# Experts' stage of a sparse layer: TensorE's program written out, with one register load per block

## The chip, the cores and the metric

The kernel runs on one core of a Trainium2 chip. The metric is the device time of one execution in microseconds (us); for a kernel it is the median of several runs. One execution of each kernel is also recorded by the hardware profiler, and all rows shown here are from that one.

## The reference

The input is a float32 tensor of 4 x 2048 tokens with 256 channels, and all products are to be computed at float32 accuracy. Cut to what matters:

```python
x = x + layernorm(attn(layernorm(x), w_lin))      # a convolution of 31 taps, its weights a softmax per token and head
x = x + layernorm(ffn(layernorm(x), ...))

def ffn(x):                                       # x: 8192 tokens x 256
    shared = silu(x @ shared_w_gate.T) * (x @ shared_w_up.T) @ shared_w_down.T      # inner width 704
    shared = shared * sigmoid(x @ shared_gate_w.T)
    rw, sel = top_k(softmax(x @ gate_w.T), 2)     # 2 of 16 experts for each token
    combine = scatter(rw / rw.sum(-1), sel)
    g, h = split(einsum('nd,edf->nef', x, w_gate_up))      # 128 + 128 columns per expert
    out = einsum('nef,efd,ne->nd', silu(g) * h, w_down, combine)
    return out + shared
```

The change lies in the last two lines of the experts' part: the products with `w_gate_up` and `w_down`.

## The kernel before, in words

The program has four stages with a barrier of all engines between them: attention; routing together with a first part of the shared network; the experts; the rest of the shared network with the combination of everything (`shared_and_combine`).

Routing sorts the 16384 pairs of token and expert by expert and cuts them into blocks of 128 rows, each for one expert only; NBK is 144 blocks. It leaves in SBUF the row numbers of each block (`ids`) and, in a row of int32 on one partition, the expert of each block (`block_expert`, with 12 zeros behind the 144 values). The weights of all 16 experts are held in SBUF too, each as two float32r tensors: `eh` holds the rounded values and `el` what rounding left. A product at float32 accuracy is then made of three: high by high, high by low, low by high.

The experts' stage (`experts`, from line 1111) works through the blocks like this:

- GpSimd gathers the 128 rows of a block (`xg`, an indirect DMA, line 806), up to eight blocks ahead.
- TensorE transposes them (`turn_x`, two transposes, line 1184). ScalarE rounds the result to `xh` (line 1234), and VectorE forms the rest `xl` (line 1252).
- TensorE multiplies by gate and up weights (`gate_up`, line 1208): for each half `c` of the channels three products, six in all. The weights loaded into the array are the rows of x; what streams through is the expert's slice of `eh` or `el`, at an address computed from the register that holds the expert's number.
- ScalarE takes the silu (line 1238) and VectorE the product (line 1256). TensorE transposes that (`turn_h`, line 1215), and ScalarE and VectorE split it into `ehh` (line 1242) and `ehl` (line 1260).
- TensorE multiplies by the down weights (`down`, three products, line 1222). VectorE copies the result out (line 1265) and SyncE stores it (line 1162).

The order is written out by hand. A step n does, on TensorE, `turn_x` of block n + 2, `turn_h` of block n - 1, `gate_up` of block n + 1 and `down` of block n - 2, in this order. So `gate_up` of a block comes one step after its `turn_x`, and `down` of a block three steps after its `gate_up`. Each engine has the same helper, `steps` (line 1137): the steps -2 to 1 are written out, then a hardware loop of 17 turns holds eight steps each (R = 8), then the steps 138 to 145 are written out again. Line 1140 is the loop itself. GpSimd alone has no loop.

TensorE needs each block's expert number in a register. Before, it loads twelve registers at once (`load_experts`, line 1189): before the first step, at the beginning of each turn of the loop and once behind the loop, 19 loads in all. `find` hands out the loaded registers to the blocks. A turn needs eight new ones and four that the steps before had already (for `down` of the last blocks).

Of the kernel before, what the change touches and what calls it, by code (L numbers as in the profile page):

```python
# [32 lines left out]
FF, E, MF = 704, 16, 128  # L33
# [8 lines left out]
NBK = NBLK + 1  # L42
# [762 lines left out]
def gather_rows(nc, to, yn_d, ids, b):  # L805
    return nc.gpsimd.indirect_dma_start(out=to, out_offset=None, in_=yn_d.rearrange("n p c -> (n p) c"),  # L806
                                        in_offset=bass.IndirectOffsetOnAxis(ap=ids[:, b:b + 1], axis=0))
# [303 lines left out]
def experts(nc, eh, el, xg, xg_in, x_full, ids, first_d, yn_d, yg_d, ident, ones, block_expert, pb):  # L1111
    with ExitStack() as ctx:
        def sb(name, shape, dt=F32):
            return ctx.enter_context(nc.sbuf_tensor(name, shape, dt))

        def sem(name):
            return ctx.enter_context(nc.semaphore(name))
        R = 8
        xg2 = sb("xg2", [P, R // 2, C])
        xh = sb("xh", [P, 2, C], F32R)  # L1120
        xl = sb("xl", [P, 2, C], F32R)
        sg = sb("esg", [P, 2, P])
        hm = sb("ehm", [P, 2, P])
        hh = sb("ehh", [P, 2, P], F32R)
        hl = sb("ehl", [P, 2, P], F32R)
        yo = sb("yo", [P, R, C])
        names = "xh_ok xl_ok gu_full sg_ok hm_ok ht_full hh_ok hl_ok y_full yo_ok".split()
        s = {n: sem("e_" + n) for n in names}
        s["x_full"] = x_full
        yo_out = [sem(f"e_yo_out{k}") for k in range(R)]  # L1130
        block = ctx.enter_context(nc.Block())
        px, pg, ph, py = pb[0:2], pb[2:4], pb[4:6], pb[6:8]
        AHEAD = R - 2
        FROM = 2
        TO = FROM + (NBK - AHEAD - FROM) // R * R

        def steps(eng, step, enter=None):
            for n in range(-2, FROM):
                step(n, n % R)
            with eng.Fori(0, (TO - FROM) // R) as i:  # L1140
                if enter:
                    enter(i * R + FROM, FROM % R)
                for u in range(R):
                    step(i * R + FROM + u, (FROM + u) % R)
            if enter:
                enter(TO, TO % R)
            for n in range(TO, NBK + 2):
                step(n, n % R)

        def rows(r):  # L1150
            return xg[:, r] if r < R // 2 else xg2[:, r - R // 2]

        def parts(n, r, *work):
            for ahead, f in work:
                if not isinstance(n, int) or 0 <= n + ahead < NBK:
                    f(n + ahead, (r + ahead) % R)

        @block.sync
        def _(sp):
            def store(b, r):  # L1160
                sp.wait_ge(s["yo_ok"], b + 3)
                sp.dma_start(yg_d[bass.ds(b * P, P)] if not isinstance(b, int) else yg_d[b * P:b * P + P], yo[:, r]
                             ).then_inc(yo_out[r], 16)
            for k in range(R):
                sp.dma_start(first_d[k], ones[:, 0:4]).then_inc(yo_out[k], 16)
            steps(sp, lambda n, r: parts(n, r, (-2, store)))
            for k in range(R):
                sp.wait_ge(yo_out[k], 16 + NBK // R * 16)

        @block.gpsimd  # L1170
        def _(po):
            for b in range(R // 2, NBK):
                if b >= R:
                    po.wait_ge(s["x_full"], b + 1)
                gather_rows(nc, rows(b % R), yn_d, ids, b).then_inc(xg_in[b % R], 16)

        @block.tensor
        def _(pe):
            pe.sem_inc(s["x_full"], R)

            def turn_x(b, r):
                pe.wait_ge(xg_in[r], (b - r) * (16 // R) + 16)
                for c in range(CC):
                    ins = nc.tensor.transpose(px[r % 2][:, c * P:(c + 1) * P], rows(r)[:, c * P:(c + 1) * P], ident[:])  # L1184
                ins.then_inc(s["x_full"], 1)
            held, loaded = {}, []

            def load_experts(b):
                loaded[:] = nc.values_load_multi_w_load_instructions(
                    block_expert[0:1, bass.ds(b, R + 4)], engines=(mybir.EngineType.PE,), min_val=0, max_val=E - 1,  # L1190
                    skip_runtime_bounds_check_because="routing clamps every block's expert to 0 .. E - 1")[1]

            def find(_, r):
                if loaded:
                    held[r] = loaded.pop(0)

            def enter(n, r):
                load_experts(n - 2)
                for k in range(-2, 2):
                    find(n + k, (r + k) % R)  # L1200

            def gate_up(b, r):
                e = held[r]
                pe.wait_ge(s["xl_ok"], b + 3)
                j = 0
                for c in range(CC):
                    for a, w in ((xh, eh), (xh, el), (xl, eh)):
                        ins = nc.tensor.matmul(pg[r % 2][:, 0:2 * MF], a[:, r % 2, c * P:(c + 1) * P],  # L1208
                                               w[:, bass.ds(e, 1), c * C:(c + 1) * C], start=(j == 0), stop=(j == 5))
                        j += 1  # L1210
                ins.then_inc(s["gu_full"], 1)

            def turn_h(b, r):
                pe.wait_ge(s["hm_ok"], b + 3)
                nc.tensor.transpose(ph[r % 2][:, 0:P], hm[:, r % 2], ident[:]).then_inc(s["ht_full"], 1)

            def down(b, r):
                e = held[r]
                pe.wait_ge(s["hl_ok"], b + 3)
                pe.wait_ge(s["yo_ok"], b + 1)  # L1220
                for j, (a, w) in enumerate(((hh, eh), (hh, el), (hl, eh))):
                    ins = nc.tensor.matmul(py[r % 2][:, 0:C], a[:, r % 2], w[:, bass.ds(e, 1), 2 * C:3 * C],
                                           start=(j == 0), stop=(j == 2))
                ins.then_inc(s["y_full"], 1)
            load_experts(0)
            steps(pe, lambda n, r: parts(n, r, (2, turn_x), (-1, turn_h), (1, gate_up), (-2, down), (2, find)), enter)

        @block.scalar
        def _(act):
            act.preload_act_table(ACT.Silu)  # L1230

            def x_high(b, r):
                act.wait_ge(s["x_full"], b + 1 + R)
                nc.scalar.activation(xh[:, r % 2], px[r % 2][:, 0:C], ACT.Copy).then_inc(s["xh_ok"], 1)  # L1234

            def silu(b, r):
                act.wait_ge(s["gu_full"], b + 1)
                nc.scalar.activation(sg[:, r % 2], pg[r % 2][:, 0:MF], ACT.Silu).then_inc(s["sg_ok"], 1)

            def h_high(b, r):  # L1240
                act.wait_ge(s["ht_full"], b + 1)
                nc.scalar.activation(hh[:, r % 2], ph[r % 2][:, 0:P], ACT.Copy).then_inc(s["hh_ok"], 1)
            steps(act, lambda n, r: parts(n, r, (2, x_high), (-1, h_high), (1, silu)))

        @block.vector
        def _(ve):
            for name in ("xl_ok", "hm_ok", "hl_ok", "yo_ok"):
                ve.sem_inc(s[name], 2)

            def x_low(b, r):  # L1250
                ve.wait_ge(s["xh_ok"], b + 1)
                nc.vector.tensor_tensor(xl[:, r % 2], px[r % 2][:, 0:C], xh[:, r % 2].bitcast(F32), ALU.subtract).then_inc(s["xl_ok"], 1)  # L1252

            def gated(b, r):
                ve.wait_ge(s["sg_ok"], b + 1)
                nc.vector.tensor_tensor(hm[:, r % 2], sg[:, r % 2], pg[r % 2][:, MF:2 * MF], ALU.mult).then_inc(s["hm_ok"], 1)

            def h_low(b, r):
                ve.wait_ge(s["hh_ok"], b + 1)
                nc.vector.tensor_tensor(hl[:, r % 2], ph[r % 2][:, 0:P], hh[:, r % 2].bitcast(F32), ALU.subtract).then_inc(s["hl_ok"], 1)  # L1260

            def leave(b, r):
                ve.wait_ge(s["y_full"], b + 1)
                ve.wait_ge(yo_out[r], (b - r) * (16 // R) + 16)
                nc.vector.tensor_copy(yo[:, r], py[r % 2][:, 0:C]).then_inc(s["yo_ok"], 1)
            steps(ve, lambda n, r: parts(n, r, (2, x_low), (-1, h_low), (1, gated), (-2, leave)))
# [203 lines left out]
```

## Time and profile before

| | us |
|---|---|
| median of 3 runs | 1089.03 (1088.56 to 1089.05) |
| the profiled execution | 1088.95 |
| its span, first to last instruction | 1086.9 |
| TensorE matmuls busy | 959.6 (88%) |
| VectorE busy | 861.3 (79%) |
| ScalarE busy | 557.3 (51%) |
| GpSimd busy | 489.6 (45%) |

The span is a little shorter than the time of the execution, as what lies before the first and after the last instruction isn't in it. Busy time is the sum of the durations of an engine's instructions, without overlaps. PE is TensorE's matmuls and PEld its weight loads; they overlap, and matmuls are pipelined, so two that start 0.12 us apart can each have a duration of 0.28 us. The start times tell the pace.

### The profile page before, as it was taken

The page shows a single profiled execution, that of the slowest core. Times are in us where ns is not written, and L with a number is a line of the kernel's source. Part 1 is how long each engine was busy: PE and PEld are TensorE (multiplying, and loading weights), DVE is VectorE, ACT ScalarE, POOL GpSimd, SP SyncE. Part 2 cuts the span into 40 slices and gives each one's busy share as a digit, 9 for nine tenths or more (in the row PEclk, how much of TensorE's full clock was granted, in tenths as well). Part 3 has the DMA queues.
Part 4 walks back from the last instruction along what each step waited for, and adds up shares of the span by engine and source line. Part 5 has one row for each costly group of instructions (what it writes and reads, how often), then busy time and mean ns, then how long its engine had stood idle before and what let it go on. Part 6 is the DMA issues. An engine that isn't in the chain of part 4 may idle for free. (4 is left out here: it accounts for less than half of the span.)

```text
span 1086.9 us, 27047 instructions
## 1 busy us (share of the span) xinstructions
PE 959.6 (88%) x9256; PEld 843.6 (78%) x9257; DVE 861.3 (79%) x2402; ACT 557.3 (51%) x1314; POOL 489.6 (45%) x715
## 2 busy tenths in 40 slices
PE   5998898998899768887897999999998799999995
PEld 4767787886788657766676998999987688888884
DVE  5977998797999668888885688788884578878777
ACT  5994445899144532333235455555553345554553
POOL 4452556421355400000002665566644786777762
PEclk9998999999899769899989899999999899999998
DMA  5532678633468630221123655555575465555541
GB/s 170 170 96 70 185 228 253 197 123 84 116 191 241 204 117 15 79 72 49 49 68 107 153 172 170 165 168 171 171 156 174 150 180 175 175 169 189 157 145 49
DMA packets 154723, 156.86 MB, mean 144 GB/s; under 512 B 52480, under 2 KB 134528, under 8 KB 154624
## 3 DMA queue, kind: packets, MB, share of 16 engines
q1 hardware_dynamic: 136048, 112.40, 33.5%
q0 software_dynamic: 13056, 35.67, 12.3%
q10 hardware_dynamic: 5520, 7.47, 2.3%
q8 instruction: 62, 1.02, 0.4%
q14 instruction: 37, 0.30, 0.1%
HBM read 91.38 MB, written 64.11 MB: 143 GB/s over the span
## 5 line engine op out<-in xcount | busy, mean ns | idle before, releaser
L806 POOL DMA_INDIRECT xg<-yn_scratch,ids x144 | 136.9, 951 | 282.9 <-DVE ids L1046 188.0
L1334 POOL DMA_INDIRECT cy<-expert_rows,slots x128 | 146.1, 1141 | 54.1 <-issue 35.8
L765 PE MATMUL bank<-yh,gh 128*128 128x512 f32 x352 | 144.8, 411 | 19.4 <-DVE s_hf L745 9.1
L647 PE MATMUL bank<-xbd,am 128*32 128x68 f32 x4096 | 138.2, 304 | 11.0 <-DMA xbd<-xn_scratch 6.6
L765 PE MATMUL bank<-yl,gh 128*128 128x512 f32 x352 | 142.3, 404 | 0.0
L765 PE MATMUL bank<-yh,gl 128*128 128x512 f32 x352 | 141.9, 403 | 0.0
L647 PEld LDWEIGHTS bank<-xbd,am 128*32 128x32 f32 x4096 | 122.8, 129 | 18.5 <-issue 8.8
L765 PEld LDWEIGHTS bank<-yh,gh 128*128 128x128 f32 x352 | 68.8, 195 | 33.8 <-DVE s_hf L745 7.9
L1208 PE MATMUL bank<-eh,xh 128*128 x288 | 94.0, 327 | 0.6 <-DVE xl L1252 0.6
L1252 DVE TENSOR_TENSOR xl<-bank,xh 128x256 fp32r<-128x256 f32 x144 | 61.1, 424 | 34.1 <-ACT xh L1234 27.0
L1234 ACT ACTIVATE xh<-bank 128x256 fp32r<-128x256 f32 x144 | 55.2, 384 | 61.5 <-PE bank L1184 61.0
L436 DVE TENSOR_TENSOR am<-probs,mask 128x512 f32<-128x512 f32 x128 | 80.0, 687 | 8.4 <-ACT probs L529 7.6
L1208 PE MATMUL bank<-el,xh 128*128 x288 | 83.0, 288 | 0.0
L725 ACT ACTIVATE s_hh<-s_hf 128x512 fp32r<-128x512 f32 (+1 forms) x36 | 22.7, 632 | 115.8 <-DVE s_hf L745 115.8
L1208 PE MATMUL bank<-eh,xl 128*128 x288 | 81.7, 284 | 0.0
L765 PEld LDWEIGHTS bank<-yh,gl 128*128 128x128 f32 x352 | 68.6, 195 | 16.9
L765 PEld LDWEIGHTS bank<-yl,gh 128*128 128x128 f32 x352 | 68.8, 195 | 12.3
L543 ACT ACTIVATE av<-av,shift,rstd 128x256 f32<-128x256 f32 x64 | 35.0, 594 | 82.7 <-POOL shift L347 82.7
L780 PE MATMUL bank<-dh,c_hh 128*128 128x256 f32 x240 | 67.3, 285 | 9.8 <-DVE c_hh L751 9.5
L368 POOL TENSOR_TENSOR x<-av,xr 128x256 f32<-128x256 f32 x64 | 46.9, 754 | 63.0 <-ACT yn L552 59.7
L725 ACT ACTIVATE c_hh<-c_hf 128x512 fp32r<-128x512 f32 (+1 forms) x60 | 38.0, 633 | 71.9 <-DVE c_hf L745 71.9
L745 DVE TENSOR_TENSOR c_hf<-c_sg,bank 128x512 f32<-128x512 f32 (+1 forms) x60 | 41.2, 687 | 42.0 <-ACT c_sg L723 41.5
(191 smaller groups left out, 2865.7 us busy)
## 6 DMA issues: line engine op xcount, KB each, us to landing
expert_rows<-yo SPq DMA_DIRECT2D x144, 128.0 KB, 1.8
xbd<-xn_scratch SPq DMA_DIRECT2D x128, 72.0 KB, 2.3
xt<-xp SPq DMA_DIRECT2D x32, 256.0 KB, 2.7
xn_scratch<-xn SPq DMA_DIRECT2D x64, 128.0 KB, 2.7
xr<-x SPq DMA_DIRECT2D x32, 256.0 KB, 3.6
x_scratch<-x SPq DMA_DIRECT2D x32, 256.0 KB, 3.5
yn_scratch<-yn SPq DMA_DIRECT2D x32, 256.0 KB, 3.7
ynt_scratch<-ynt SPq DMA_DIRECT2D x32, 256.0 KB, 4.4
```

What stands on the lines that cost most here:

```text
L368: nc.gpsimd.tensor_tensor(x2[:, q, t], av[:, q, t], xr[:, q, t], ALU.add).then_inc(s["x2_ok"], 1)
L436: nc.vector.tensor_tensor(am[:, q, g], probs[:, bass.ds(i * CB, CB), g, None, :].to_broadcast([P, CB, 2, J]), mask[:, None].to_broadcast([ ...
L647: ins = nc.tensor.matmul(pso[q][t][J * b:J * b + J, g * MW:(g + 1) * MW], am[:, q, g, e, side], xbd[:, q, e + side, :, g], start=(g == 0 a ...
L725: self.nc.scalar.activation(self.hh[0:f, g], self.hf[0:f, k], ACT.Copy).then_inc(self.s["hh_ok"], 1)
L745: self.nc.vector.tensor_tensor(self.hf[0:f, k], self.sg[0:f, k], up, ALU.mult).then_inc(self.s["hf_ok"], 1)
L765: ins = self.nc.tensor.matmul(self.pb[2 * k + half][:], w[:, c, col:col + P], y[:, n % 2, c, :], start=(j == 0), stop=(j == 5))
L780: ins = self.nc.tensor.matmul(o, a[:, g, t * P:(t + 1) * P], w[:, m, :], start=(m == 0 and t % 2 == 0 and j == 0), stop=(m == FT - 1 and j ...
L806: return nc.gpsimd.indirect_dma_start(out=to, out_offset=None, in_=yn_d.rearrange("n p c -> (n p) c"), in_offset=bass.IndirectOffsetOnAxis ...
L1208: ins = nc.tensor.matmul(pg[r % 2][:, 0:2 * MF], a[:, r % 2, c * P:(c + 1) * P], w[:, bass.ds(e, 1), c * C:(c + 1) * C], start=(j == 0), s ...
L1234: nc.scalar.activation(xh[:, r % 2], px[r % 2][:, 0:C], ACT.Copy).then_inc(s["xh_ok"], 1)
L1252: nc.vector.tensor_tensor(xl[:, r % 2], px[r % 2][:, 0:C], xh[:, r % 2].bitcast(F32), ALU.subtract).then_inc(s["xl_ok"], 1)
L1334: nc.gpsimd.indirect_dma_start(out=y[:, r, t, j], out_offset=None, in_=yg_d, in_offset=bass.IndirectOffsetOnAxis(ap=slots[:, 2 * unit + t, ...
```

## The change

TensorE no longer uses `steps`: its 148 steps are written out. Thresholds of its waits become constants by that. A load of one register comes before the first step; then each `gate_up` holds the load for the next block, between its third and fourth product. `load_experts` and `enter` go. All other engines keep their loops, and what is computed stays the same.

```diff
-        def steps(eng, step, enter=None):
+        def steps(eng, step):
             for n in range(-2, FROM):
                 step(n, n % R)
             with eng.Fori(0, (TO - FROM) // R) as i:
-                if enter:
-                    enter(i * R + FROM, FROM % R)
                 for u in range(R):
                     step(i * R + FROM + u, (FROM + u) % R)
-            if enter:
-                enter(TO, TO % R)
             for n in range(TO, NBK + 2):
                 step(n, n % R)
...
-            held, loaded = {}, []
-
-            def load_experts(b):
-                loaded[:] = nc.values_load_multi_w_load_instructions(
-                    block_expert[0:1, bass.ds(b, R + 4)], engines=(mybir.EngineType.PE,), min_val=0, max_val=E - 1,
-                    skip_runtime_bounds_check_because="routing clamps every block's expert to 0 .. E - 1")[1]
-
-            def find(_, r):
-                if loaded:
-                    held[r] = loaded.pop(0)
-
-            def enter(n, r):
-                load_experts(n - 2)
-                for k in range(-2, 2):
-                    find(n + k, (r + k) % R)
+            held = {}
+
+            def find(b):
+                held[b] = nc.values_load_multi_w_load_instructions(
+                    block_expert[0:1, b:b + 1], engines=(mybir.EngineType.PE,), min_val=0, max_val=E - 1,
+                    skip_runtime_bounds_check_because="routing clamps every block's expert to 0 .. E - 1")[1][0]
 
             def gate_up(b, r):
-                e = held[r]
+                e = held[b]
                 pe.wait_ge(s["xl_ok"], b + 3)
                 j = 0
                 for c in range(CC):
...
                                                w[:, bass.ds(e, 1), c * C:(c + 1) * C], start=(j == 0), stop=(j == 5))
                         j += 1
+                        if j == 3 and b + 1 < NBK:
+                            find(b + 1)
                 ins.then_inc(s["gu_full"], 1)
...
             def down(b, r):
-                e = held[r]
+                e = held.pop(b)
...
-            load_experts(0)
-            steps(pe, lambda n, r: parts(n, r, (2, turn_x), (-1, turn_h), (1, gate_up), (-2, down), (2, find)), enter)
+            find(0)
+            for n in range(-2, NBK + 2):
+                parts(n, n % R, (2, turn_x), (-1, turn_h), (1, gate_up), (-2, down))
```

## Rows read from the trace of the kernel before

**Rows 1.** The page: its first line and engine busy times.

```profile
span 1086.9 us, 27047 instructions
...
PE 959.6 (88%) x9256; PEld 843.6 (78%) x9257; DVE 861.3 (79%) x2402; ACT 557.3 (51%) x1314; POOL 489.6 (45%) x715
```

**Rows 2.** Engines by stretches: stretch, length, busy of each, PEclk, DMA share, GB/s.

```profile
100.00:150.00 50.00, 44.95 (x1189) 40.85 (x1184) 47.84 (x139) 18.65 (x48) 28.39 (x51) 1.00 0.67 186
150.00:200.00 50.00, 45.19 (x864) 39.81 (x857) 41.97 (x132) 28.82 (x80) 30.88 (x69) 0.93 0.82 249
...
606.00:815.00 209.00, 194.41 (x1625) 190.31 (x1624) 168.50 (x543) 112.25 (x406) 124.97 (x133) 1.00 0.58 168
```

**Rows 3.** Who waited for whom, 596 to 826 us: total, times, longest.

```profile
POOL xg L806 <- PE bank L1184: 75.3, 122, 2.1
...
PEld bank L1184 <- issue: 22.9, 18, 4.8
```

**Rows 4.** Timeline of TensorE's weight loads: start, us, line; idle time before it.

```profile
617.28 0.20 PEld L1184 LDWEIGHTS bank<-ident,xg 128*128 128x128 f32 x2 [1.15 <-issue]
...
621.49 0.25 PEld L1184 LDWEIGHTS bank<-ident,xg 128*128 128x128 f32 x2
...
622.88 0.25 PEld L1184 LDWEIGHTS bank<-ident,xg 128*128 128x128 f32 x2
...
623.56 0.19 PEld L1208 LDWEIGHTS bank<-eh,xh 128*128 128x128 f32 x1
...
624.29 0.24 PEld L1184 LDWEIGHTS bank<-ident,xg 128*128 128x128 f32 x2
...
627.07 0.24 PEld L1184 LDWEIGHTS bank<-ident,xg 128*128 128x128 f32 x2
...
628.34 0.19 PEld L1222 LDWEIGHTS bank<-eh,ehl 128*128 128x128 f32 x1
629.65 0.20 PEld L1184 LDWEIGHTS bank<-ident,xg 128*128 128x128 f32 x2 [1.13 <-issue]
...
803.33 0.20 PEld L1184 LDWEIGHTS bank<-ident,xg 128*128 128x128 f32 x2 [1.06 <-issue]
```

**Rows 5.** Line 1189 in several stretches: ns min/median/max, first and last start (us).

```profile
L1189 PEldq TENSOR_LOAD <-block_expert x19: 852/1072/1851, 596.1 to 814.3; - x19
...
L1189 PEldq TENSOR_LOAD <-block_expert x1: 1851/1851/1851, 596.1 to 596.1; - x1
...
L1189 PEldq TENSOR_LOAD <-block_expert x1: 872/872/872, 603.4 to 603.4; - x1
...
L1189 PEldq TENSOR_LOAD <-block_expert x1: 1095/1095/1095, 628.4 to 628.4; - x1
...
L1189 PEldq TENSOR_LOAD <-block_expert x11: 1054/1073/1095, 628.4 to 752.4; - x11
```

**Rows 6.** The chain that ended last, behind the stage: start, us, what.

```profile
827.59 0.94 POOL cy L1334
...
869.52 3.20 issue
```

**Rows 7.** Timeline of weight loads behind the loop.

```profile
815.13 0.20 PEld L1184 LDWEIGHTS bank<-ident,xg 128*128 128x128 f32 x2 [0.49 <-issue]
```

**Rows 8.** The sequencer's own instructions, by line, in three stretches and in all.

```profile
L1208 PEldq FUSED_REGOPS  x2: 46/46/46, 624.3 to 624.5; - x2
...
L1208 PEldq FUSED_REGOPS  x2: 46/46/46, 816.5 to 816.7; - x2
...
L1222 PEldq ALU_OP  x1: 32/32/32, 817.2 to 817.2; - x1
...
L1140 PEldq COMPARE_BRANCH  x17: 83/215/232, 615.6 to 814.1; - x17
```

**Rows 9.** Timeline of VectorE, the low part of x.

```profile
623.83 0.42 DVE L1252 TENSOR_TENSOR xl<-bank,xh 128x256 fp32r<-128x256 f32 x1
...
630.54 0.42 DVE L1252 TENSOR_TENSOR xl<-bank,xh 128x256 fp32r<-128x256 f32 x1 [1.19 <-ACT xh L1234]
```

## The prediction

> **What bounds the kernel now.** I read the page first: 1086.9 us of span, with TensorE busy for 88% of it, more than any other engine [rows 1]. Then I read stretches, because the change touches one stage alone. The experts' stage runs from about 596 to 826 us; between 606 and 815 us TensorE is busy 194.4 of 209.0 us and its granted clock is 1.00, that is 2.4 GHz [rows 2]. So something takes 7% of TensorE's time there, and the view of who waited for whom names it: 18 waits of the weight loads ahead of the transposes of line 1184, put down to "issue", 22.9 us [rows 3]. The reader should see that no other engine is named: TensorE's own instruction stream is late. The other row says who follows whom: GpSimd waits for the same transposes 122 times, so its gathers go at TensorE's pace.
>
> The timeline shows the pattern. Inside a turn of the loop, the first transpose of one step and that of the next start 1.39 to 1.40 us apart (621.49, 622.88, 624.29); across the loop's edge it is 2.58 us (627.07 to 629.65), with 1.13 us in which no weight load runs [rows 4]. In that gap stands one instruction of line 1189, the load of twelve registers: 1.095 us from 628.4 [rows 5]. It begins when the queue ahead of the array holds the last products only (the last weight load starts at 628.34), so nearly all of it is bare. The stage ends in a barrier, and behind it GpSimd's gathers start at 827.59 and carry the chain until TensorE takes over near 870 [rows 6]. Nothing there began before the barrier, so a shorter or longer experts' stage moves the end by the same amount.
>
> **Part by part, the removed edges.** First transposes at the sixteen turns' edges start at 617.28, ..., 803.33: fifteen intervals, 186.05 / 15 = 12.40 us for eight blocks [rows 4]. Eight dense steps are 8 x 1.395 = 11.16 us (627.07 less 621.49 is 5.58 us for four). An edge costs 1.24 us, sixteen cost 19.9 us. The seventeenth load, behind the loop, leaves a gap of 0.49 us [rows 7]: 0.5 us. The load at the loop's entry (603.4, 0.87 us [rows 5]) costs nothing: at half clock a block of products lasts longer than it. Sum of what can go: 20.4 us. The very first load is on the path too: 1.85 us with TensorE idle [rows 5]. One register in place of twelve saves between 0 and 1.8 us of it; it is the first of its kind and cold, so I take 0.3 us.
>
> **Thresholds and branches.** The register arithmetic for waits and the branch itself (0.22 us in the median, 0.08 where not taken [rows 8]) are issued while the sequencer has time to spare, or are in the 1.24 us already. Written-out code has no such arithmetic: 0 us, between -0.1 (sequencer's slack gone) and 0. The longer program must be fetched; the attention stage, which is also written out, runs 1189 matmuls and 1184 weight loads in 50 us, 47 a microsecond [rows 2], and a block here needs 24 with some ten register instructions in 1.39 us, 25 a microsecond. 0 us, and up to 1 us if a fetch comes late now and then.
>
> **The other engines' loops** stay. Today their edges fall near TensorE's gap; later they fall amid dense work. The low part of x ends at 624.25 and the first products of the next step are released at 624.3 [rows 8, 9], with their weight load some 0.1 to 0.3 us later, so a hundred nanoseconds lost by VectorE's branch can reach TensorE. Seventeen edges by 0 to 0.15 us: 0 to 2.5 us, I take 0.8 us.
>
> **The new loads** decide. There are 144 of them, one per block, in place of 19. Each sits between the third and the fourth product of a block; the sequencer does nothing else while it lasts, so the question is its duration, X. No row has a load of one register. Bounds from the nearest rows: twelve registers took 0.85 us at least (the last one, with no gathers beside it) and 1.07 us in the median of the nineteen [rows 5]. If the price is all per register, X is 0.07 to 0.09 us; if none of it is, 0.85 to 1.07 us.
>
> What a given X does is a cycle over two steps. (1) From the release of a block's products (sequencer) to the load: 0.24 us, the distance of the two address instructions of line 1208 (816.5, 816.7 [rows 8]). (2) The load, X. (3) From the load's end to the next weight load with one address instruction between: 0.15 us, as 629.50 to 629.65 today [rows 4, 5]. (4) Fourth product to the next transpose: 0.72 us (623.56 to 624.29 [rows 4]). (5) Transpose, ScalarE's copy, VectorE's difference, release of the step after: 629.65 to 630.96 and some 0.04 us, 1.35 us where nothing presses [rows 4, 9]. Two periods are at least 0.24 + X + 0.15 + 0.72 + 1.35, so the period is at least 1.23 + X/2. I add 0.02 for the dense case, where step 5 takes 1.40 us (622.88 to 624.3): 1.25 + X/2. The sequencer alone needs 0.84 us for a block (816.5 to 817.2, and the pushes of three transposes), and 0.06 us around a load: 0.90 + X. TensorE's own work is 1.395 us. The period is the largest of the three.
>
> So up to X = 0.29 us the load is free: the queue and the chain cover it. Above it each 0.1 us costs 0.05 us a block, 7 us over 141 blocks, and above 0.70 us twice that. The gain of 20.4 us is eaten when the period reaches 1.395 + 20.4/141 = 1.540 us, at X = 0.58 us.
>
> Which X? The eleven loads between 628 and 753 us lie between 1.054 and 1.095 us [rows 5], and are 0.2 us longer than the quiet one. Twelve small delays add up to so narrow a band more easily than one round trip under traffic does. I take a twelfth of 1.07, 0.09 us, and a fixed part like that of the other control instructions with work in them, 0.08 to 0.22 us [rows 8]: X = 0.25 us.
>
> The Trainium skill speaks against this, and its pages against each other. "DMA: Bandwidth & Descriptors", section "Latency and other measured facts", has a floor of about 600 ns for a tensor load; by it the sum would be a small loss, about 2 us, and more under traffic. "Runtime: NRT & Kernel Launch", section "Instruction fetch mechanics", has about 200 ns per register; by that twelve would take 2.4 us, and the trace has 0.85 to 1.10 once warm, so as a figure it does not hold here, though its kind of cost (per register) is the one that I take.
>
> **Sum.** -19.9 - 0.5 - 0.3 + 0.8 + 0 (loads, fully covered, since 1.25 + 0.125 is under 1.395) = -19.9 us. The profiled execution took 1088.95 us, 2.05 us more than its span; 1088.95 - 19.9 = 1069.05 us. The median of the runs is 1089.03, 0.08 above. As the cover at X = 0.25 is thin (0.04 us from its end) I add 0.7 us (a period longer by 0.005 us, 141 times): 1069.8 us.
>
> **The rivals.**
> - *The load is mostly a fixed price.* Two thirds or more of the quiet 0.85 us, so X is 0.63 us up to 0.85. The period is then 1.565 us, and 1.75 us at the top by the sequencer. (1.565 - 1.395) x 141 = 24.0, less 20.4: +4 us, 1093 us; at the top 50.1 - 20.4 = +30 us, 1119 us; with 1.07 us even the period 1.97 and +61 us, 1150 us. It decides from X = 0.58 us. For it: the first load took 1.85 us, so a load is no plain register instruction. Against it: the narrow band. TensorE would also be busy only 89% or less; stretches of attention busy 45.2 of 50 us were granted 0.93 [rows 2], which could add some us. The skill's floor of a tensor load, named above, is this rival.
> - *Half and half.* X between 0.30 and 0.53 us: a period of 1.40 to 1.515 us, +1 to +17 us on -20.4: 1069 to 1086 us.
> - *The edges' gain isn't kept*: with the gap gone VectorE or GpSimd sets the pace. GpSimd's gather takes 0.94 us with 0.3 between two, waiting 75.3 us in all for TensorE [rows 3], so it could go at 1.25 us; VectorE is busy 168.5 of 209.0 us [rows 2], 81%, and 87% of a stage shortened to 195. The price would be all of 20 us, 1089 us. Little speaks for it.
>
> **How the numbers follow.** Chances: forecast (X up to 0.30) 0.47; half and half 0.14; X of 0.53 to 0.63, which lands within 2 us of before, 0.07; mostly fixed 0.30; gain not kept 0.02. No change here means within 0.2%, 2.2 us, about what a measurement of this kernel can tell. Faster is 0.47 + 0.14 less 0.01 = 0.60, within 0.2% 0.07 + 0.02 = 0.09, slower 0.31 (0.30 and 0.01 for a clock that falls). The range begins at 1066 us (the first load saves 1.8, the other edges cost nothing) and reaches to the fixed price at X = 0.7 us, 1.60 us a step, +9 us: 1098 us. Left out are some 0.03 below and 0.16 above. Forecast's own range: 1066 to 1074 us.
>
> **What would show it.** A row of TENSOR_LOAD for one register, x144: near 0.25 us is right, 0.6 and more is the first rival. First transposes 1.39 to 1.42 us apart all through, with no gap at every eighth. Waits on "issue" ahead of line 1184 down from 18 to 1 or 2. If instead the fourth product of each block starts late by some hundred nanoseconds and the steps lie 1.5 us or more apart, step 2 of the cycle was longer than I take. Gaps of TensorE put down to VectorE's xl at every eighth block would show the other loops' edges. The stages ahead of 596 us and behind the barrier must have the same lengths; if not, the sum is wrong in its frame.

## The result, and the profile after

The changed kernel takes 1080.39 us in the median of five runs (1078.07 to 1083.44), the kernel before 1089.05 (1088.56 to 1089.88): a ratio of 0.9925, interval 0.9904 to 0.9945. It is faster by 0.75%, where 1.8% was forecast.

The page of the changed kernel, first line and engines:

```profile
span 1078.5 us, 26898 instructions
...
PE 965.1 (89%) x9256; PEld 847.5 (79%) x9256; DVE 861.5 (80%) x2402; ACT 557.2 (52%) x1314; POOL 491.1 (46%) x715
```

The change did what it says. The waits on "issue" ahead of the transposes (now line 1180) fell from 18 to the one at the stage's start. In their place stand 15 ahead of the products of line 1195. The view of waits of the changed kernel, 596 to 826 us:

```profile
PEld bank L1195 <- issue: 4.4, 15, 1.0
PEld bank L1180 <- issue: 4.0, 1, 4.0
```

That view shows only the gaps in which no weight load ran. The loss is greater and lies in the steps' length, from the first transpose of one step to that of the next. This is the timeline of its weight loads:

```profile
688.86 0.24 PEld L1180 LDWEIGHTS bank<-ident,xg 128*128 128x128 f32 x2
...
689.42 0.19 PEld L1195 LDWEIGHTS bank<-eh,xl 128*128 128x128 f32 x1
689.93 0.19 PEld L1195 LDWEIGHTS bank<-eh,xh 128*128 128x128 f32 x1 [0.33 <-issue]
...
690.64 0.24 PEld L1180 LDWEIGHTS bank<-ident,xg 128*128 128x128 f32 x2
...
692.07 0.24 PEld L1180 LDWEIGHTS bank<-ident,xg 128*128 128x128 f32 x2
```

The weight loads of a block's third and fourth product start 0.51 us apart here instead of 0.12, and the step takes 1.78 us (688.86 to 690.64); the next takes 1.43. What stands between is one register load, 0.517 us from 689.3. First its row, then all 144, then those before and from 607 us on (line 1185 of the changed kernel; ns min/median/max):

```profile
L1185 PEldq TENSOR_LOAD <-block_expert x1: 517/517/517, 689.3 to 689.3; - x1
...
L1185 PEldq TENSOR_LOAD <-block_expert x144: 297/382/1088, 597.9 to 811.2; - x144
...
L1185 PEldq TENSOR_LOAD <-block_expert x6: 298/304/1088, 597.9 to 606.5; - x6
...
L1185 PEldq TENSOR_LOAD <-block_expert x138: 297/384/564, 608.0 to 811.2; - x138
```

So X is 0.30 us in the first blocks and 0.30 to 0.56 us later, 0.40 us on the mean of blocks 10 to 137. Those rows answer to [rows 5]. The busy share warns of nothing. Engines of the changed kernel between 606 and 806 us:

```profile
606.00:806.00 200.00, 199.28 (x1620) 193.82 (x1619) 167.45 (x540) 111.90 (x405) 126.47 (x134) 1.00 0.62 177
```

TensorE is "busy" for 199.3 of 200 us, against 194.4 of 209 in [rows 2], while a step takes 1.485 us on the mean instead of the 1.395 inside a turn of the loop before. A product's record lasts 0.28 us where two start 0.12 us apart, and the late fourth one has 0.38, so most of the delay is hidden under records. Counting blocks per microsecond tells the pace, the share does not.

The time by parts, from starts in both traces: first to last block's transpose, 221.26 us before and 211.95 after (-9.3); the first load 1.85 and 1.09 (-0.8); up to the barrier ahead of the stage +1.8, in code that the change does not touch; from the last transpose to the end 267.6 and 267.5 (-0.1). Together -8.4 us, the difference of the spans.

### The profile page after: what moved, and what is told of

Its sections match the earlier page's. It is cut to its first block and busy times, and to the rows that moved or that the text cites. A ratio compares the mean times of both kernels' runs of the same rounds, so it can differ in the third digit from the quotient of the medians.

```text
span 1078.5 us, 26898 instructions
## 1 busy us (share of the span) xinstructions
PE 965.1 (89%) x9256; PEld 847.5 (79%) x9256; DVE 861.5 (80%) x2402; ACT 557.2 (52%) x1314; POOL 491.1 (46%) x715
## 5 line engine op out<-in xcount | busy, mean ns | idle before, releaser
L1195 PE MATMUL bank<-eh,xh 128*128 x288 | 100.1, 348 | 1.5 <-DVE xl L1242 0.8
```

## The experiments

Times of one kernel differ between chips by some us, so each run is compared by its ratio with the kernel before on the same chip. Where no ratio is given there is a single execution, and only its trace is read. "Stage" is the time from the first to the last block's first transpose; the lines of the transposes give it. "Steps" are those of blocks 10 to 137. The edits are cut to what matters.

**No loads at all.** All blocks use the register of the first.

```diff
-                e = held[b]
+                e = held[0]
...
-                        if j == 3 and b + 1 < NBK:
-                            find(b + 1)
...
-                e = held.pop(b)
+                e = held[0]
```

> Leaves out all loads of an expert's number but the first: every block is multiplied with the first block's expert. The instructions are otherwise those of the changed kernel. Theory A: steps of 1.395 us throughout, the 0.089 us that a step has on the mean beyond that times 137 steps go, 12 us: 1068 us. This is also the term of 20 us for the removed edges by itself. Theory C: the steps stay near 1.48 us or are late at every eighth, 1075 to 1080 us.

Measured: 1068.43 us, 0.9810 (0.9770 to 0.9849). Each step takes 1.392 to 1.400 us. The transposes' row, of this kernel and of the changed one:

```profile
L1180 PEld LDWEIGHTS bank<-ident,xg x288: 137/139/224, 598.0 to 798.8; 128*128 128x128 f32 x144
```

```profile
L1180 PEld LDWEIGHTS bank<-ident,xg x288: 137/140/224, 599.0 to 811.1; 128*128 128x128 f32 x144
```

The stage is 200.6 us, 20.6 less than before and 11.3 less than with the loads. So the edges were worth what was forecast, the other engines' loops (in the kernel before, VectorE's branch takes 0.05 to 0.07 us) and the fetching of the long program cost nothing that can be seen, and the loads cost 11.3 us.

**The load ahead of the wait for xl.**

```diff
                 e = held[b]
+                if b + 1 < NBK:
+                    find(b + 1)
                 pe.wait_ge(s["xl_ok"], b + 3)
...
-                        if j == 3 and b + 1 < NBK:
-                            find(b + 1)
```

> The one-register load moves from between the third and fourth product to ahead of gate_up's wait for xl, behind the pushes of the transposes. Theory A (the cycle: a load delays only what follows it in TensorE's program, and its price is what sticks out of time in which the sequencer has nothing to do): the sequencer waits there for xl some 0.45 us of every step, the load has a mean of 0.39 us, so it is covered but for the longest ones; steps of 1.395 to 1.41 us, 1068 to 1071 us. Theory B (a load costs its price wherever it stands, because it stops the queue ahead of the array): 1080 us, as with the load amid the products. Theory C (what was lost comes from the other engines' loop edges or from fetching the written-out code): 1078 to 1081 us too, with late steps at every eighth.

Measured: 1066.39 us, 0.9813 (0.9780 to 0.9847). Stage 199.8 us, steps of 1.392 to 1.400 us: as without any load. The number of loads is the same; only their place differs. Its transposes and its loads from 608 us:

```profile
L1180 PEld LDWEIGHTS bank<-ident,xg x288: 137/139/229, 593.4 to 793.2; 128*128 128x128 f32 x144
...
L1185 PEldq TENSOR_LOAD <-block_expert x133: 296/301/440, 608.4 to 792.6; - x133
```

B and C fall. The loads are also shorter here, 0.306 us on the mean, which no theory had said. So this run by itself leaves open how much is the place and how much the shorter load; the runs without stores and with chosen counts, below, part the two.

**Two loads amid the products.** The line `find(b + 1)` stands twice.

> Two loads of one register, one behind the other, between the third and the fourth product, X = 0.85 us instead of 0.39. Theory A: the period is the larger of 1.25 + X/2 = 1.675 us and 0.90 + X = 1.75 us, so 0.27 us more in 141 steps: 1118 us. A straight line through no load and one load (12 us for 0.39 us) gives 1094 us instead.

Measured: 1079.82 us, 0.9931 (0.9909 to 0.9953). It tests nothing: the trace holds 144 loads, not 287, so the unused one had gone from the program. As a repetition of the changed kernel it gives its time again.

```profile
L1185 PEldq TENSOR_LOAD <-block_expert x144: 296/382/1090, 593.0 to 807.9; - x144
```

**Behind the down products**, ahead of the next step's transposes.

```diff
-                parts(n, n % R, (2, turn_x), (-1, turn_h), (1, gate_up), (-2, down))
+                parts(n, n % R, (2, turn_x), (-1, turn_h), (1, gate_up), (-2, down), (2, lambda b, r: find(b) if b else None))
```

> The one-register load stands behind the down products, ahead of the next step's transposes. Theory A in its mended form (a load's time counts in full only between the release of a block's products and the next transposes, when it stands amid products that the array hasn't in its queue; elsewhere the sequencer's 0.5 us of spare time in a step take it): 0.31 + 0.06 us fit in, steps of 1.395 us, 1066 to 1069 us. Rival (the load delays the transposes, and by the chain over two steps half of it comes out as with the load amid the products): steps near 1.45 us, 1078 us.

Measured: 1068.78 us, 0.9809 (0.9778 to 0.9840), steps of 1.392 to 1.400 us, stage 199.6 us. The mended theory holds: two places around the wait are free for a load of 0.31 us, the one amid the products is not.

**Writing out alone**: batches of twelve (`find` now loads R + 4 registers) at the old place, and none amid the products.

```diff
-                    block_expert[0:1, b:b + 1], engines=...
+                    block_expert[0:1, b:b + R + 4], engines=...
...
-                        if j == 3 and b + 1 < NBK:
-                            find(b + 1)
...
+                if FROM <= n <= TO and (n - FROM) % R == 0:
+                    find(n - 2)
                 parts(n, n % R, (2, turn_x), (-1, turn_h), (1, gate_up), (-2, down))
```

> TensorE's program written out, but the loads as before the change: twelve registers at once ahead of every eighth step, at the place of the loop's edge. Tells the writing-out from the placing of loads. Theory A (the queue ahead of the array runs dry because of the load): branch and loop arithmetic go, so the load starts some 0.45 us earlier while the queue is still fuller, and 16 edges keep 1.24 - 0.45 = 0.8 us each: 1081 us, steps of 1.395 us between. Rival (the edge is the branch's price: after a taken branch the code must be fetched anew, and the load's 1.07 us beside the 0.85 us of the one behind the loop is that too): the load falls to 0.85 us and the edges keep 0.5 us or less: 1076 us.

Measured: 1074.11 us, 0.9878 (0.9855 to 0.9900), better than the change itself. Its loads, then its timeline at an edge:

```profile
L1185 PEldq TENSOR_LOAD <-block_expert x17: 844/849/867, 612.5 to 795.9; - x17
```

```profile
634.57 0.24 PEld L1180 LDWEIGHTS bank<-ident,xg 128*128 128x128 f32 x2
...
635.84 0.19 PEld L1210 LDWEIGHTS bank<-eh,ehl 128*128 128x128 f32 x1
636.29 0.20 PEld L1180 LDWEIGHTS bank<-ident,xg 128*128 128x128 f32 x2 [0.27 <-issue]
...
637.65 0.24 PEld L1180 LDWEIGHTS bank<-ident,xg 128*128 128x128 f32 x2
```

The edge's two steps take 1.72 and 1.36 us; 3.08 less 2.79 leaves 0.3 us for an edge, 1.24 before. Both theories have a part, and a third thing went that neither had. The starts of the sequencer's instructions give it: from the last address instruction of a step to the load 0.11 us instead of 0.60 (branch and loop arithmetic), the load 0.85 us instead of 1.07, from the load's end to the release of the next products 0.08 us instead of 0.39 (register arithmetic for the waits). Whether the load is shorter for want of a taken branch, as the rival has it, or because it meets no store (below), no run shows for the batch.

**The loop kept, its batch moved** behind the turn's first transposes.

```diff
+                if due:
+                    enter(*due.pop())
                 e = held[r]
                 pe.wait_ge(s["xl_ok"], b + 3)
...
-            steps(pe, lambda n, r: parts(...), enter)
+            steps(pe, lambda n, r: parts(...), lambda n, r: due.append((n, r)))
```

> The kernel before with one edit: the loop stays, and its load of twelve registers moves from ahead of the turn's first transposes to between them and the wait for xl. Theory A: the sequencer has some 0.45 us to spare there and the queue holds the transposes, so an edge costs about 0.6 us instead of 1.24: 1078 us. If place did not matter: 1088 us.

Measured: 1089.27 us, 1.0006 (0.9987 to 1.0024): no gain. Its loads and the edge:

```profile
L1189 PEldq TENSOR_LOAD <-block_expert x16: 974/1055/1274, 613.7 to 799.6; - x16
```

```profile
626.16 0.14 PEld L1219 LDWEIGHTS bank<-ident,ehm 128*128 128x128 f32 x1
627.37 0.19 PEld L1212 LDWEIGHTS bank<-eh,xh 128*128 128x128 f32 x1 [1.06 <-issue]
```

The gap only moved behind the transposes. I had counted the sequencer's spare 0.45 us for the load, but at an edge the loop's own instructions (add, branch of 0.22 us, address) stand ahead and spend it. From the last address instruction of a step to the release of the next products it takes 2.08 us on the mean at the edges of the kernel before, 2.06 here and 1.05 in the written-out run, and an edge costs 1.24, 1.24 and 0.30 us. So in all three some 0.8 us of that distance are free and the rest counts, on whichever side of the transposes the load stands. Writing out shortens the distance by branch and arithmetic, and so frees the time that hides a load. A loop that keeps its branch and has one-register loads ahead of the wait was not tried.

**What makes the load longer.** Stores held back until behind the last block:

```diff
-                sp.dma_start(yg_d[...], yo[:, r]).then_inc(yo_out[r], 16)
+                sp.sem_inc(yo_out[r], 16)
...
+            for b in range(NBK):
+                sp.dma_start(yg_d[b * P:b * P + P], yo[:, b % R]).then_inc(late, 16)
```

> The changed kernel without SyncE's stores while the blocks are worked on: all 144 are issued in a burst behind the last block, from whatever the buffers then hold, so its whole time says nothing. Looked at: the duration of the one-register loads, 0.30 us in the first ten and 0.30 to 0.56 us from then on. If the stores' traffic is what the load meets, it is 0.30 us throughout and the steps fall to about 1.44 us; if it is the gathers', it stays as it was, 0.39 us on the mean.

And no gathers after the first eight blocks:

```diff
-            for b in range(R // 2, NBK):
-                if b >= R:
-                    po.wait_ge(s["x_full"], b + 1)
+            for b in range(R // 2, R):
...
-                pe.wait_ge(xg_in[r], (b - r) * (16 // R) + 16)
+                if b < R:
+                    pe.wait_ge(xg_in[r], 16)
```

> The changed kernel with the gathers of the first eight blocks alone; the later blocks use their rows again. Looked at: the duration of the one-register loads. If the gathers are what the load meets: 0.30 us throughout, steps of about 1.44 us by the cycle as measured (1.285 + X/2), TensorE's stage 7 us shorter: 1074 us. If the stores are: 0.39 us as before.

Each is a single execution, for its trace. The loads without stores, then without gathers:

```profile
L1188 PEldq TENSOR_LOAD <-block_expert x140: 295/301/316, 600.2 to 799.3; - x140
```

```profile
L1184 PEldq TENSOR_LOAD <-block_expert x135: 297/435/564, 608.2 to 809.8; - x135
```

It is the stores (128 KB from SBUF per block). Without them X is 0.30 us throughout, and the step takes 1.431 us on the mean, 1.436 by the measured cycle below; the stage takes 204.9 us (the whole 1139.86 us, with the stores in a burst at the end). Without gathers X stays long, 0.44 us on the mean, the step takes 1.504 us and the whole 1079.3 us. So of the 11.3 us that the loads cost, 4.3 are a load of 0.30 us at this place, and 7.0 its lengthening by stores.

Why the place matters to X too is read from the traces alone, no run moved the stores. Amid the products a load starts 0.57 to 0.86 us behind the start of a store's issue, and 101 of 134 take over 0.33 us; ahead of the wait it starts mostly 1.15 to 1.37 us behind, and 5 of 134 do. The batches at the written-out edge start 1.2 us behind a store and take 0.85 us; those of the loop start 0.2 to 0.3 us behind, last through the busy time and take 1.07 us in the median.

**The price by the number of registers.** First amid the products, in turn 1, 2, 4 and 8 from places 4k, 4k + 1, 4k + 2, 4k + 3; the whole took 1165.09 us, where 1090 was expected.

```diff
+                k = (1, 2, 4, 8)[b % 4]
                 held[b] = nc.values_load_multi_w_load_instructions(
-                    block_expert[0:1, b:b + 1], engines=...
+                    block_expert[0:1, b:b + k], engines=...
```

> The loads at their place take 1, 2, 4 and 8 registers in turn, of which the first alone is used. Price per register from twelve at 1.07 and one at 0.39 us: 0.062 us. So 0.39, 0.45, 0.58, 0.82 us if the price is a fixed part of 0.33 us and an equal one for each register; a step at some count (all of one fetch for one price) would show as two equal durations. Time near 1090 us by the cycle (mean X 0.56 us).

```profile
L1186 PEldq TENSOR_LOAD <-block_expert x1: 322/322/322, 600.5 to 600.5; - x1
...
L1186 PEldq TENSOR_LOAD <-block_expert x1: 535/535/535, 602.7 to 602.7; - x1
...
L1186 PEldq TENSOR_LOAD <-block_expert x1: 1107/1107/1107, 605.3 to 605.3; - x1
...
L1186 PEldq TENSOR_LOAD <-block_expert x1: 2158/2158/2158, 607.3 to 607.3; - x1
```

A miss: eight registers take about 2 us where twelve had taken 0.85. So the counts were taken again with the places chosen, ahead of the wait:

> The loads stand ahead of the wait for xl and take 12, 1, 2, 2, 4, 4, 2, 1, 8, 1, 2, 2, 4, 4, 2, 1 registers in turn, from the block's own place in the list; the first alone is used. Loads of 2, 4 and 8 that began at odd places took 0.24 us for each register more; twelve that began at a multiple of eight took 0.85 us. If the price goes by pieces of 16 bytes that a load touches, loads of 4, 8 and 12 from a multiple of four take some 0.35, 0.6 and 0.85 us, and those of 4 from an odd place 1.0 us. If it goes by the number of registers alone, 4 take 1.0 us wherever they begin and 8 take 1.95, and twelve at 0.85 us stay unexplained. The whole time says little.

Four from 12, four from 13, eight from 24, twelve from 16, two from 18:

```profile
L1186 PEldq TENSOR_LOAD <-block_expert x1: 339/339/339, 613.7 to 613.7; - x1
...
L1186 PEldq TENSOR_LOAD <-block_expert x1: 1002/1002/1002, 615.0 to 615.0; - x1
...
L1186 PEldq TENSOR_LOAD <-block_expert x1: 601/601/601, 632.1 to 632.1; - x1
...
L1186 PEldq TENSOR_LOAD <-block_expert x1: 857/857/857, 619.9 to 619.9; - x1
...
L1186 PEldq TENSOR_LOAD <-block_expert x1: 547/547/547, 622.9 to 622.9; - x1
```

From a place that is a multiple of four, 4, 8 and 12 registers take 0.34, 0.60 and 0.86 us: 0.26 us for each four (16 bytes) and 0.08 fixed. Others take some 0.23 us for each register and 0.07 fixed: 0.30, 0.54, 1.00. In 11 of the 16 positions at least eight of the nine loads agree within 0.03 us; three positions of two registers and the two of four from an odd place spread more, by 0.08 to 0.41 us. A group of four costs about what one register does.

This run also says how much is hidden ahead of the wait. Two of its steps, with twelve registers (0.86 us from 619.9) and with eight (0.60 us from 632.1):

```profile
620.31 0.25 PEld L1180 LDWEIGHTS bank<-ident,xg 128*128 128x128 f32 x2
...
621.94 0.24 PEld L1180 LDWEIGHTS bank<-ident,xg 128*128 128x128 f32 x2
...
632.55 0.24 PEld L1180 LDWEIGHTS bank<-ident,xg 128*128 128x128 f32 x2
...
633.95 0.24 PEld L1180 LDWEIGHTS bank<-ident,xg 128*128 128x128 f32 x2
```

The first takes 1.63 us, the second 1.40. From block 17 on all eight loads of eight registers (0.59 to 0.60 us) and all 32 of two that don't follow a long one (0.53 to 0.64 us) leave steps of 1.39 to 1.40 us; the seven of twelve (0.85 to 0.87 us) have steps of 1.58 to 1.65 us. So it is the place that makes a load free there, up to 0.6 us of it, and not its being short: theory A holds. Amid the products 0.30 us already cost something (1.431 us a step without stores).

**The best version**: ahead of the wait, and the very first load behind the first transposes. Against the run with the load ahead of the wait:

```diff
+                if b == 0:
+                    find(0)
                 e = held[b]
                 if b + 1 < NBK:
                     find(b + 1)
                 pe.wait_ge(s["xl_ok"], b + 3)
...
-            find(0)
```

> The load ahead of the wait for xl as in the best run so far, and the very first load (1.08 us, ahead of the stage's first transposes) moved behind the first two blocks' transposes, where TensorE waits 1.4 us for xl anyway. Theory A: 1.0 us less than with the load ahead of the wait alone, 1065 to 1067 us; visible in the trace as the distance from the barrier to the first transpose, less in a time of runs that spread by 3 us. If the first products come later by as much, nothing is gained.

Measured: 1065.84 us, 0.9792 (0.9768 to 0.9816). From TensorE's arrival at the barrier to the first product it takes 5.9 us instead of 6.7 (the run with the load ahead of the wait). In time the two can't be told apart. Either beats both kernels.

## Why the prediction was wrong

The direction and the cycle over two steps were right, the size was not. The spans differ by -8.4 us: the edges -20.6, the first load -0.8, the new loads +11.3, the stages ahead +1.8, behind -0.1.

- *Removed edges, -20.4 us*: right. Without loads the stage is 20.6 us shorter, with whatever the other engines' loops cost in it.
- *First load, -0.3 us*: -0.8 us; cold, one register takes 1.09 us.
- *Other engines' loops, +0.8 us*: nothing measurable; VectorE's branch takes 0.05 to 0.07 us, and the steps of the run without loads have no late eighth.
- *Thresholds, branches, fetching, 0 us*: held as a term of its own, with one thing missed. I put branch and arithmetic among what the 1.24 us of an edge contains and did not see how large their share is: written out with the very same batches, an edge keeps 0.3 us. Branch and loop arithmetic take 0.49 us of the sequencer there, the arithmetic for the waits 0.31, the longer load 0.22.
- *The new loads, 0 us (0.7 with the margin)*: this is the step that failed. They cost 11.3 us. X was taken as 0.25 us and is 0.40, and the cover that I gave it ended at 0.29. The cycle itself is the right one. Its terms, means of blocks 10 to 137 of the changed kernel, with the forecast's in brackets: release to load 0.26 (0.24); load 0.40 (0.25); load's end to the fourth product 0.17 (0.15); fourth product to the next transposes 0.73 (0.72); transposes to release 1.41 (1.39). The sum is 2.97 us for two steps, 1.485 for one, and 1.485 us is what the trace has. Forecast were 2.75 and so 1.375, under TensorE's own 1.395. Of the 0.11 us between, 0.075 are X, and 0.035 the small rest. That small rest also moved the end of the cover: the period is 1.285 + X/2 with the measured terms, and passes 1.395 at X = 0.22 us, so that even the 0.25 us forecast would not have been free.

The five terms follow one another around two steps, so their sum is two steps whatever the mechanism. What bears the cycle out is, first, that four of them stay the same within 0.01 us when X changes: with X of 0.30 us (no stores), 0.40 (the changed kernel) and 0.44 (no gathers) the step takes 1.431, 1.485 and 1.504 us. Second, in 118 of the 128 blocks the release comes within 0.06 us behind the end of VectorE's xl; in the other ten the sequencer itself is late. One such release, at 692.04 us, 0.04 us behind the end of xl (VectorE's timeline, then the sequencer's row of line 1195):

```profile
691.58 0.42 DVE L1242 TENSOR_TENSOR xl<-bank,xh 128x256 fp32r<-128x256 f32 x1
...
L1195 PEldq FUSED_REGOPS  x1: 46/46/46, 692.0 to 692.0; - x1
```

It is also the sign that the prediction named for a load that is too long: the fourth product late by some hundred nanoseconds.

Why was X wrong? I took a twelfth of the batch's price for one register. The batch behaves as if it were read in three aligned pieces of 0.26 us; a single register costs almost a piece and the fixed part, 0.30 us. The bounds (0.07 to 1.07 us) held it; my choice inside them rested on a narrow band that said nothing on this question. And 0.10 us more comes from the stores; the same rows had two prices for a batch (0.85 and 1.07 us) without my asking at which moment of a step the new loads would fall.

The rival "half and half" (X from 0.30 to 0.53 us, 1069 to 1086 us), with 0.14, is what happened. The range held the median.

Of the two rules of the Trainium skill: the floor of about 600 ns for a tensor load ("DMA: Bandwidth & Descriptors", "Latency and other measured facts") does not hold for this load from SBUF, which takes 0.30 us. The 200 ns per register ("Runtime: NRT & Kernel Launch", "Instruction fetch mechanics"), which the page gives for the runtime's own register loads, is near the 0.23 us of registers read one by one here, though not near aligned groups of four. I had dismissed it as a figure with the batch of twelve.

## What to carry to other kernels

In this kernel the instructions that TensorE's sequencer carries out itself are free only in time in which it has nothing else to do. So look for the wait at which it stands idle in each step, and put them just ahead of it or behind the last push rather than between the release of a group of products and the group's end (1.395 against 1.485 us a step here). One allowance covers all of them together, branches and loop arithmetic included: a batch of 0.85 us costs 0.3 us in written-out code, and a batch in the loop, of 1.07 us, costs 1.24. When a batch is to be replaced by single loads, the price of one is not the batch's divided by its count: measure it.

## What the runs showed of the hardware

A register load from SBUF on TensorE costs 0.07 to 0.08 us and then 0.23 us for each register, or 0.26 us for each four where it begins at a multiple of four places of the row and takes 4, 8 or 12; the first in this stage takes 0.8 us more (one register, 1.09 us) or 1.0 us more (twelve, 1.85 us). Ahead of the wait up to 0.6 us of it is hidden in a step of 1.395 us. With a store of 128 KB from SBUF in each step, a load of one register amid the products takes from 0.30 up to 0.56 us, and without the stores 0.30 to 0.32; leaving out the gathers into SBUF does not shorten it. Which of a store's parts does it (its reads of SBUF or its descriptors) stays open.
